# Zero rows under the 16-row and 1-row products of two convolution layers and the bias rows of an attention

## The reference

```
# L0: self-attention over 256 pixels, with 16 channels for queries and keys
q, k = Wq x + bq, Wk x + bk                # 16 x 256 per image
v = Wv x + bv                              # 128 x 256
attention = softmax(q^T k)                 # 256 x 256 per image
out = gamma * (v attention^T) + x
x = relu(batchnorm(Wf out))
# L1: gate = sigmoid(mean(Q K)); energy = (V gate) Qs^T  (128 x 16 per image)
attention = softmax(energy)                # 128 x 16
x = x + attention (We x + be)              # 128 x 16 times 16 x 256
# L2, attention: over the 8 images at each pixel, after a layer norm
q, k, v = rotated(t Wq + bq), rotated(t Wk + bk), t Wv + bv
t = t + attn(q, k, v) Wo + bo
```

## Time and profile before

| | |
|---|---|
| time, median of 3 runs | 605.85 us (605.59 to 612.24) |
| the profiled execution | 606.89 us |
| its span in the profile | 605.1 us |
| busy share of the span | PE 82%, DVE 68%, POOL 47%, ACT 43% |
| mean granted clock of PE | 0.761 |
| first block (L0, L1) | 0 to 80.2 us |
| second block (L2's attention) | 80.2 to 162 us |

### The profile page before, as it was taken

How to read it: one execution, slowest core, us unless ns; L and a number is a source line. 1 busy time by engine, 2 the same in 40 slices (tenths; PEclk the granted TensorE clock), 3 DMA queues, 4 the chain that set the end, 5 groups by cost and what they waited for, 6 DMA issues and landing times. The chain is left out here.

```text
span 605.1 us, 9967 instructions
## 1 busy us (share of the span) xinstructions
PE 499.0 (82%) x3062; PEld 394.4 (65%) x3062; DVE 408.4 (68%) x1115; ACT 260.8 (43%) x538; POOL 285.4 (47%) x270
## 2 busy tenths in 40 slices
PE   8998995998668999999527899999957797777642
PEld 4785653968653899999516788888846355655431
DVE  2639459998978448644358688888887875555534
ACT  4532134400220675554234688888842033333314
POOL 1094429788633777777312021111121177777750
PEclk9698577898857999999856555555555799888985
DMA  6000060000280111212230000000005011112226
GB/s 232 1 1 2 0 240 38 1 0 2 69 279 9 49 54 54 49 51 52 63 107 1 1 1 2 0 0 0 2 0 140 0 44 51 51 52 53 53 64 185
DMA packets 26507, 31.06 MB, mean 51 GB/s; under 512 B 3105, under 2 KB 21538, under 8 KB 26338
## 3 DMA queue, kind: packets, MB, share of 16 engines
q1 hardware_dynamic: 21474, 20.29, 10.3%
q0 software_dynamic: 4992, 10.23, 6.5%
HBM read 20.16 MB, written 10.36 MB: 50 GB/s over the span
## 5 line engine op out<-in xcount | busy, mean ns | idle before, releaser
L1103 POOL DMA_INDIRECT xg<-rows_in,idx x78 | 76.3, 978 | 36.7 <-issue 21.0
L1109 POOL DMA_INDIRECT rows_out<-yo,idy x78 | 76.8, 985 | 29.4 <-issue 18.3
L1161 ACT ACTIVATE hraw<-ps 128x512 f32<-128x512 f32 (+1 forms) x78 | 38.3, 491 | 79.9 <-PE ps L1269 79.9
L1472 DVE TENSOR_TENSOR hidden<-ps,hidden 128x512 fp32r<-128x512 f32 (+1 forms) x78 | 43.3, 555 | 42.2 <-ACT hidden L1168 42.2
L1290 PE MATMUL ps<-wHL,hidden 128*128 x234 | 70.1, 351 | 0.6 <-DVE hidden L1472 0.4
L1293 PE MATMUL ps<-wHL,hidden 128*128 x234 | 54.5, 233 | 0.0
L1480 DVE TENSOR_REDUCE yo<-ps 128x128 f32<-128x256 f32 x78 | 32.6, 418 | 23.8 <-DMA rows_out<-yo,idy 13.2
L1154 ACT ACTIVATE xa<-ps 128x128 fp32r<-128x128 f32 x78 | 21.8, 280 | 61.0 <-PE ps L1255 61.0
L1290 PEld LDWEIGHTS ps<-wHL,hidden 128*128 128x128 f32 x234 | 45.1, 193 | 3.6 <-issue 1.5
L1293 PEld LDWEIGHTS ps<-wHL,hidden 128*128 128x128 f32 x234 | 45.4, 194 | 0.0
L1596 POOL CAST vp<-v3f 128x256 bf16<-128x256 f32 x8 | 3.7, 462 | 85.6 <-ACT s L1627 85.6
(11 more groups left out here) (287 smaller groups left out, 1325.8 us busy)
## 6 DMA issues: line engine op xcount, KB each, us to landing
wraw<-in_ex SPq DMA_DIRECT2D x2, 2048.0 KB, 9.9
rows_in<-both SPq DMA_DIRECT2D x8, 512.0 KB, 6.4
both<-rows_out SPq DMA_DIRECT2D x16, 256.0 KB, 4.1
wraw<-in_ex SPq DMA_DIRECT2D x1, 3072.0 KB, 12.4
w<-in_pack SPq DMA_DIRECT2D x1, 1582.0 KB, 8.0
xg<-rows_in,idx POOLq DMA_INDIRECT x78, 2.6
rows_out<-yo,idy POOLq DMA_INDIRECT x78, 2.3
xs<-in_x SPq DMA_DIRECT2D x4, 256.0 KB, 4.4
```

Of the source, the lines that this page charges most:

```text
L1103: pool.indirect_dma_start(xg[:, j % NXG, :], None, xs_d[:], bass.IndirectOffsetOnAxis(idx[:, j:j + 1], 0)).then_inc(ld[j % NXG], 16)
L1109: pool.indirect_dma_start(ys_d[:], bass.IndirectOffsetOnAxis(idy[:, j:j + 1], 0), yo[:, j % NYO, :], None).then_inc(st[j % NYO], 16)
L1161: act.activation(hraw[:, j % 2, :], ps[:, HB + j % 2, 0:hid], ACT.Gelu if layer == 0 else ACT.Silu).then_inc(z["act"], 1)
L1472: dve.tensor_tensor(hL[:, j % 2, :], ps[:, HTB + j % 2, 0:hid], hH[:, j % 2, :].bitcast(F32), ALU.subtract).then_inc(z["hL"], 1)
```

## The change

Every product that contracted over 16 rows or one row contracts over 128. The tiles `q0`, `k0`, `ke1` and `aT1` get 128 partitions; they are set to zero once at the start and then written in their first 16 rows as before, and the products read all 128. `ones` becomes `first`, a tile of 128x128 with ones in its first row and zeros elsewhere, and the bias products read all rows of `bb2` and `bo2`. The zeros are written by DVE (`q0`, `k0`, at the head of its list) and POOL (`first`, `ke1`, `aT1`), and the engines that write into these tiles wait for that; the counts of `s_set_v` go up by two. The title under which the change was made adds "on top of the single read of the expert numbers", which is in both kernels.

```diff
-        ones = sb("ones", [1, P])
+        first = sb("first", [P, P])
...
-        q0 = own("q0", [KD, L, CH])
-        k0 = own("k0", [KD, L, CH])
+        q0 = own("q0", [P, L, CH])
+        k0 = own("k0", [P, L, CH])
...
-        ke1 = own("ke1", [KD, L, CH])
+        ke1 = own("ke1", [P, L, CH])
...
-        aT1 = own("aT1", [KD, L, 2, P])
+        aT1 = own("aT1", [P, L, 2, P])
...
             for g in range(2):
-                pe.matmul(ps[:, KB2 + g, :].rearrange("p (i n) -> p i n", i=4), ones[:], bb2[0:1, 4 * g:4 * g + 4, P:2 * P], start=True, stop=False)
+                pe.matmul(ps[:, KB2 + g, :].rearrange("p (i n) -> p i n", i=4), first[:], bb2[:, 4 * g:4 * g + 4, P:2 * P], start=True, stop=False)
...
             chp.done(pool.memset(halfs[:], -0.5))
-            chp.done(pool.memset(ones[:], 1.0))
+            chp.done(pool.memset(first[:], 0.0))
+            chp.wait()
+            chp.done(pool.memset(first[0:1], 1.0))
             pool.memset(still[:], 0.0).then_inc(s_still, 1)
             chp.done(pool.memset(onesb[:], 1.0))
             chp.done(pool.memset(onesPb[:], 1.0))
+            pool.memset(ke1[:], 0.0).then_inc(s_still, 1)
+            pool.memset(aT1[:], 0.0).then_inc(s_still, 1)
             pool.wait_ge(s_w, 16)
...
-            pe.wait_ge(s_set_v, 2)
+            pe.wait_ge(s_set_v, 4)
...
-            act.wait_ge(s_set_v, 3)
+            act.wait_ge(s_set_v, 5)
             act.preload_act_table(ACT.Exp)
+            act.wait_ge(s_still, 3)
...
-                act.activation(q0[:, p, :], bank(p, 0)[0:KD], ACT.Identity, bias=wc("bq0", rows=KD)).then_inc(m["qk0"], 1)
+                act.activation(q0[0:KD, p, :], bank(p, 0)[0:KD], ACT.Identity, bias=wc("bq0", rows=KD)).then_inc(m["qk0"], 1)
...
         def _(dve):
             chv.engine = dve
+            dve.memset(q0[:], 0.0).then_inc(s_set_v, 1)
+            dve.memset(k0[:], 0.0).then_inc(s_set_v, 1)
             dve.wait_ge(s_w, 16)
...
             dve.wait_ge(s_set_p, 1)
-            dve.wait_ge(s_set_v, 2)
+            dve.wait_ge(s_set_v, 4)
...
                 dve.wait_ge(m["a1p"], p + 1)
-                dve.tensor_copy(aT1[:, p], bank(p, 1)[0:KD, 0:2 * P].rearrange("p (b c) -> p b c", b=2)).then_inc(m["aT1"], 1)
+                if p == 0:
+                    dve.wait_ge(s_still, 3)
+                dve.tensor_copy(aT1[0:KD, p], bank(p, 1)[0:KD, 0:2 * P].rearrange("p (b c) -> p b c", b=2)).then_inc(m["aT1"], 1)
...
-                    pe.matmul(ps[:, FB2[s] + g, :].rearrange("p (i n) -> p i n", i=4), ones[:],
-                              wc("bo2", rows=1)[:, None].to_broadcast([1, 4, P]), start=True, stop=False)
+                    pe.matmul(ps[:, FB2[s] + g, :].rearrange("p (i n) -> p i n", i=4), first[:],
+                              wc("bo2")[:, None].to_broadcast([P, 4, P]), start=True, stop=False)
```

More of the change, by code:

```diff
@@ L398, in _ @@
         def _(act):
-            act.wait_ge(s_set_v, 3)
+            act.wait_ge(s_set_v, 5)
             act.preload_act_table(ACT.Exp)
+            act.wait_ge(s_still, 3)
             def queries_keys(p):
                 act.wait_ge(m["qkp"], p + 1)
-                act.activation(q0[:, p, :], bank(p, 0)[0:KD], ACT.Identity, bias=wc("bq0", rows=KD)).then_inc(m["qk0"], 1)
-                act.activation(k0[:, p, :], bank(p, 0)[2 * KD:3 * KD], ACT.Identity, bias=wc("bk0", rows=3 * KD)[2 * KD:]).then_inc(m["qk0"], 1)
+                act.activation(q0[0:KD, p, :], bank(p, 0)[0:KD], ACT.Identity, bias=wc("bq0", rows=KD)).then_inc(m["qk0"], 1)
+                act.activation(k0[0:KD, p, :], bank(p, 0)[2 * KD:3 * KD], ACT.Identity, bias=wc("bk0", rows=3 * KD)[2 * KD:]).then_inc(m["qk0"], 1)
             def exponentials(p):
@@ L422, in keys1 @@
                 act.wait_ge(m["kep"], p + 1)
-                act.activation(ke1[:, p, :], bank(p, 0)[0:KD], ACT.Identity, bias=wc("be1", rows=KD)).then_inc(m["ke"], 1)
+                act.activation(ke1[0:KD, p, :], bank(p, 0)[0:KD], ACT.Identity, bias=wc("be1", rows=KD)).then_inc(m["ke"], 1)
             def gate_exp(p):
```

## The result

The changed kernel took 600.48 us (median of 4 runs, 598.99 to 601.17), the kernel before 606.44; the ratio is 0.990, 95% interval 0.986 to 0.994. That is 6 us less, within the two per cent that count as no change here, and clear of the runs' own spread. The profiled execution took 600.38 us (span 598.6) against 606.89 (span 605.1). Forecast was 601.2 us, against a median before of 605.85 from three runs; against this one, of four, the same -4.6 gives 601.8.

What follows compares the result with a forecast made beforehand. The chain of waits ends in the unedited second expert stage, so only shifts in the first 160 us count: +0.23 - 2.66 - 3.5 + 1.3 = -4.6 us, from the median 605.85 to 601.2 us, range 598.5 to 604.

Steps and rivals of the forecast that it cites:

- The mechanism: PE's clock: products over 128 rows, zeros included, hold or raise it to 1.00; 16-row products lose or miss it.
- Part 1: Set-up: the memset of `first` and its wait delay `still` and PE's first product; +0.23 us, between 0.2 and 1.1.
- The rival of a late warm-up: Set-up: DVE's memsets hold up POOL's `still`, so PE starts +3.7 us late; 606.7 us in all, chance 5%.
- Part 2: Energies: clock stays at 1.00, fourth maximum on DVE and the fused products come earlier; -2.66 us.
- Part 3: attended1 and the keys' bias: clock rises after 4.8 us of 128-row work, next stage starts earlier; -3.5 us.
- What is late next: End of the attended1 stage: DVE's last moments end it at 76.4; bias products hidden behind them by 1.4 us.
- Part 4: Start of the attention: shorter keep_busy leaves PE idle, a 3.4 us half-clock stretch follows; +1.3 us given back (0 to 4.7).
- The second sums: Low stretch at 138.5: on the path, 1.6 us lost to half clock; change left at 0, between -1.6 and +0.5.

Runs made afterwards that it cites:

- the two with one place each: Changed kernel with 128 rows only in the energies: 603.72 us, ratio 0.995; only in attended1 and the biases: 602.00 us, ratio 0.993.
- the moved subtractions: Changed kernel with four keep_busy products, POOL's low2 subtractions waiting for the attention's last layer norm step: 596.87 us, ratio 0.985.

## Why the prediction was right, step by step

**The mechanism** was right: the rows under the products, zeros too, hold and raise PE's clock. The kernel with every edit but the rows shows it, and the two with one place each. The energies show it without a second cause: at 1.00 a pair of images takes 1.73 us of PE with 16 rows as with 128, and PE is busy throughout in both, but with 16 the clock fell (three kernels) and with 128 it held (ten).

**Part 1** gave +0.39 for +0.23. `first` and its wait moved `still` by 0.26, as worked out; the two products behind the warm-up then ran longer as well (L301 0.63 us against 0.49), and the first projection came 0.50 later. What goes beyond the 0.26 belongs to the execution and not to the set-up: in the twelve profiles with this same set-up the energies begin anywhere from 14.42 to 15.63 us, the earliest with all products back at 16 rows or 1, where PE's products on `still` took 3.40 us and not 3.78. The DVE memsets took 1.76 us each, the POOL ones 1.80 and 0.94, where 1.9, 1.9 and 0.95 were taken from a POOL row; they were hidden. The rival of a late warm-up fell: `still` took 0.52 us beside DVE's memset, as it did without.

**Part 2** was right to 0.1 us: DVE's chain of maxima and normalisations set the pace, and the fused products moved with it.

**Part 3** is the term that was mis-sized, -5.5 for -3.5. The third pair's attended1 (64.96) ended at 65.99, that is 68.35 in the times of the kernel before, where 69.95 was forecast: 1.6 of the 2.0. The clock rose 3.3 us after the first attended1 product, not 4.8: I took the middle of three rises, and it came sooner than the shortest of them, 3.5. And at the same half clock one step from attended1 to the next took 2.13 us (60.72 to 62.85) instead of 2.53 (63.20 to 65.73), which the forecast did not have. The loading of weights shows why, first with all products at 16 rows or 1, then in the changed kernel:

```profile
63.53 1.35 PEld L385 LDWEIGHTS ps<-ke,aT 16*128 16x128 f32 x4 [0.42 <-issue]
...
65.53 0.10 PEld L377 LDWEIGHTS ps<-w,a 128*16 128x16 f32 x2 [0.65 <-issue]
```

```profile
60.51 1.40 PEld L385 LDWEIGHTS ps<-ke,aT 128*128 128x128 f32 x4
```

With 16 rows, and with 64, the weights of the first product behind one with another number of rows came late, after 0.42 us without loading into attended1 and 0.65 out of it; with 128 rows they loaded beside the product ahead of them. So the rows shortened this step by 0.4 us at the same clock. The other 0.4 are waits in DVE's chain behind it, which took 6.1 us for 6.5. What is late next was right: DVE's last moments (from 70.82) end the stage, and the bias products, hidden, end about a microsecond ahead.

**Part 4** was right in kind and too small, +2.9 for +1.3. The idle time came where it was forecast and the clock fell; but it stayed at 0.50 for 6.8 us, not 3.4, and nearly all of it fell on the queries and keys. Of the bias rows, costed at nothing in this part, the ones in keys_bias have an effect here after all: by keeping the clock at 1.00 they cut the cover, keep_busy, by 1.8 us; what that costs in the whole time is not shown.

**The second sums.** That their low stretch lies on the path was wrong, as the table and the moved subtractions show; costed at 0, it did not touch the sum.

The steps up to the router add up to -4.9 us, for -4.6 forecast, with two errors of opposite sign in it, -2.0 and +1.6: the mechanism was right, but that the sum came so close is luck. The other 1.6 us of the profiled executions lie behind it and were not forecast.

## What to carry to other kernels

A product that contracts over few rows can cost twice its time, and that of its neighbours, through PE's clock; a tile zeroed once and read in full costs nothing more per product (1.73 us for a pair's energies at 1.00 either way), and it pays where PE's time in that stage is on the path. Raising the clock shortens filler work too: where keep_busy products covered a wait, count them again, or the gain is given back right behind it. Ask of every stage at half clock whether PE's work ends last there (that of the second sums did not); only there does a higher clock move the end, until the next engine, DVE here, is the bound.

## What I had not expected of the hardware

Products of 64 rows held the clock at 1.00 through 7.1 us of energies, and 12.8 us of work with 64-row products among 128-row ones did not raise it; with 128 rows it rose 3.0 to 4.4 us after the first such product, in eight kernels. It fell 1.6 and 2.2 us after the first 1-row product of the bias, in the two kernels that have such products at full clock (69.0 to 70.6, 70.3 to 72.6). Where products of 16 or 64 rows stood between others of 128, the weights at each change of rows loaded late, 0.4 us in all for one step of attended1. And DVE operations of 0.27 us apiece (eight in 2.14) took 1.3 us each while POOL subtracted beside them.
